# A two-pass causal attention layer: rows of maxima turned by VectorE in SBUF, whole value matmuls and filler matmuls in the diagonal steps

## The reference, cut to what matters

```python
x = x + attention(layernorm(x))
x = x + relu(layernorm(x) @ w1 + b1) @ w2 + b2

def attention(x):                      # 16 heads, d_k = 16
    Q, K, V = rope(x @ Wq.T), rope(x @ Wk.T), x @ Wv.T
    scores = Q @ K.T / 4               # causal: -inf above the diagonal
    return softmax(scores) @ V @ Wo.T
```

## Time and profile before

| | |
|---|---|
| Median of three runs | 2168.51 us |
| The profiled execution: its own time | 2172.91 us |
| Its span, first to last instruction | 2171.2 us |
| TensorE busy | 2008.1 us, 92% of the span |
| VectorE busy | 1902.2 us, 88% |
| ScalarE busy | 1457.4 us, 67% |
| GpSimd busy | 637.1 us, 29% |
| Mean granted TensorE clock | 0.967 of full speed |

### The profile page before, as it was taken

The page is one execution under the profiler, slowest core; times in us unless marked ns, Lnnn a source line. Parts: engine busy times, 40 slices in busy tenths (PEclk is TensorE's granted clock), DMA queues, the critical chain, the costliest instruction groups (busy, mean ns, idle before and its releaser), DMA issues. The chain is left out here.

```text
span 2171.2 us, 53576 instructions
## 1 busy us (share of the span) xinstructions
PE 2008.1 (92%) x19136; PEld 790.4 (36%) x19136; DVE 1902.2 (88%) x3974; ACT 1457.4 (67%) x3092; POOL 637.1 (29%) x1265
## 2 busy tenths in 40 slices
PE   5786599999999999999999999999999969999999
PEld 3444122222222222222222222222222237766776
DVE  8998899999999999999999999999999337777775
ACT  5664078888888788888888788888887742333222
POOL 7999421120221202221121211212212123332231
PEclk9999599999999999999999999999999889999999
DMA  5567331230313303033130322303120212222220
GB/s 193 203 220 209 122 70 37 51 65 17 72 27 64 61 22 66 21 76 50 33 66 17 76 35 52 66 17 74 27 52 13 69 39 78 82 94 84 87 78 29
DMA packets 126407, 152.64 MB, mean 70 GB/s; under 512 B 17248, under 2 KB 92512, under 8 KB 125920
## 3 DMA queue, kind: packets, MB, share of 16 engines
q1 hardware_dynamic: 126176, 149.67, 26.0%
HBM read 90.12 MB, written 59.24 MB: 69 GB/s over the span
## 5 line engine op out<-in xcount | busy, mean ns | idle before, releaser
L868 ACT ACTIVATE s_prob<-s_ps 128x512 f32<-128x512 f32 (+3 forms) x2560 | 1179.3, 540 | 276.5 <-PE s_ps L723 267.3
L797 DVE TENSOR_REDUCE s_part<-s_ps 128x2 f32<-128x1024 f32 x768 | 909.1, 1222 | 42.7 <-PE s_ps L706 25.1
L742 PE MATMUL s_ps<-s_prob,s_v 128*32 128x256 f32 (+3 forms) x10240 | 744.4, 363 | 8.4 <-POOL s_prob L898 0.9
L723 PE MATMUL s_ps<-aq,ak 64*128 64x512 f16 (+3 forms) x2560 | 674.5, 355 | 7.2 <-DVE s_part L804 1.2
L706 PE MATMUL s_ps<-mk,mq 64*128 64x512 f16 (+3 forms) x2560 | 590.7, 355 | 60.4 <-DVE s_part L797 28.1
L898 POOL TENSOR_SCALAR_AFFINE_SELECT s_prob<-s_prob 128x128 f32<-128x128 f32 x1024 | 286.7, 292 | 1170.7 <-ACT s_prob L868 1158.2
L804 DVE CUSTOM_DVE_ANT_0 s_ps<-s_ps,mask_sb 128x512 f32<-128x512 f32 (+3 forms) x1024 | 472.3, 520 | 25.9 <-PE s_ps L706 20.6
L723 PEld LDWEIGHTS s_ps<-aq,ak 64*128 64x128 f16 x2560 | 180.9, 93 | 524.0 <-ACT s_prob L868 439.9
L742 PEld LDWEIGHTS s_ps<-s_prob,s_v 128*32 128x32 f32 x10240 | 202.2, 108 | 464.4 <-issue 378.3
L706 PEld LDWEIGHTS s_ps<-mk,mq 64*128 64x128 f16 x2560 | 141.0, 95 | 105.4 <-DVE s_part L797 48.9
L1166 ACT ACTIVATE s_h_f<-s_ps,s_b_s 128x512 f32<-128x512 f32 x128 | 87.9, 687 | 105.9 <-PE s_ps L1031 85.0
(11 more groups left out here) (86 smaller groups left out, 1562.1 us busy)
## 6 DMA issues: line engine op xcount, KB each, us to landing
v_scratch<-s_vst SPq DMA_DIRECT2D x32, 512.0 KB, 3.9
s_v<-v_scratch SPq DMA_DIRECT2D x16, 1024.0 KB, 10.8
att_scratch<-s_o SPq DMA_DIRECT2D x64, 256.0 KB, 2.4
aq<-qk_scratch SPq DMA_DIRECT2D x96, 128.0 KB, 4.3
ak<-qk_scratch SPq DMA_DIRECT2D x96, 128.0 KB, 6.9
s_xin<-x SPq DMA_DIRECT2D x16, 512.0 KB, 4.4
qk_scratch<-s_r_lo SPq DMA_DIRECT2D x64, 128.0 KB, 2.2
qk_scratch<-s_r_hi SPq DMA_DIRECT2D x64, 128.0 KB, 2.4
```

The costliest lines, as they stand in the source:

```text
L723: nc.tensor.matmul(ps[:, s_bank(s, j), q0:CH], ak[rows, p, j // 2, kb * P:(kb + 1) * P], aq[rows, p, j // 2, c * CH + q0:(c + 1) * CH], st ...
L742: last = nc.tensor.matmul(ps[32 * j:32 * j + 32, O_BANK, cols], v[:, p, kb, j, :], prob[:, s % 2, j, cols], start=kb == 0 and part == 0, s ...
L797: nc.vector.tensor_reduce(part[:, qt // TPC, :, pair, qt % TPC, kc], ps[:, bank_of(use):bank_of(use) + 2, 0:w], AX.X, ALU.max).then_inc(m_ ...
L868: nc.scalar.activation(prob[:, s % 2, j, q0:CH], ps[:, s_bank(s, j), q0:CH], ACT.Exp, scale=1.0 / (SQK * DK ** 0.5)).then_inc(p_done, 1)
```

## The change

- `qmax` is reduced to a tile 32 columns wide, of which 16 are used, VectorE turns it in blocks of 32x32 in SBUF (`turn_chunk`) and scales it there (`rows_out`). TensorE's `max_rows` and its two uses of the ring are gone.
- The turned tile holds a chunk's rows in four pieces of 32 queries, so `rows` now issues eight DMAs of 64-byte pieces in place of four of 256-byte pieces. `aq` gets the layout `[NC, NP, CH]`, and its loads become twelve DMAs in place of six (18 in `load_a` in place of 12).
- In all diagonal steps the order on TensorE is: scores 0 and 1, first pair of maxima, score 2, second pair of maxima, score 3, and then the value matmuls whole, in place of two halves.
- In the diagonal steps of the tail, where there are no maxima, two pairs of 512-column matmuls that nobody reads are issued in their place (`filler_pair`).

```diff
-                dst = (ops.ak if qk else ops.aq)[rows, p]
-                sp.dma_start(dst, src[jj]).then_inc(ops.a_in[p], 16)
+                if qk:
+                    sp.dma_start(ops.ak[rows, p], src).then_inc(ops.a_in[p], 16)
+                    continue
+                for jp in range(NP):
+                    sp.dma_start(ops.aq[rows, p, :, jp], src[:, jp].rearrange("r (c t) -> r c t", c=NC)
+                                 ).then_inc(ops.a_in[p], 16)
...
-        self.aq = ctx.enter_context(nc.sbuf_tensor("aq", [P, 2, NP, S], F16))
+        self.aq = ctx.enter_context(nc.sbuf_tensor("aq", [P, 2, NC, NP, CH], F16))
...
-                sp.wait_ge(m_read, NM + rows_use(i, c) + ROWS_TILES)
-                for j in range(G):
-                    row = HROWS * (j % 2) + MAXROW
-                    k = TPC * (NP * (j % 2) + j // 2)
-                    sp.dma_start(aq[row:row + 1, i % 2, j // 2, c * CH:(c + 1) * CH], nrow[k:k + TPC, c, :]
-                                 ).then_inc(rows_in[c], 16)
+                sp.wait_ge(nrow_done, NC * i + RANK[c] + 1)
+                for jj in range(2):
+                    row = HROWS * jj + MAXROW
+                    dst = aq[row:row + 1, i % 2, c].rearrange("a n (q u x) -> a u (n q) x", u=P // TURN, x=TURN)
+                    for u in range(P // TURN):
+                        k = TURN * u + NP * TPC * jj
+                        sp.dma_start(dst[:, u], nrow[k:k + NP * TPC, c, :]).then_inc(rows_in[c], 16)
...
-            def max_rows(i, c):
-                use = rows_use(i, c)
-                pe.wait_ge(qmax_done, NC * i + RANK[c] + 1)
-                pe.wait_ge(m_read, use + ROWS_TILES)
-                nc.tensor.transpose(ps[0:G * TPC, bank_of(use), 0:P], qmax[:, c, :], ident[:]
-                                    ).then_inc(m_ready, ROWS_TILES)
+            def filler_pair(p, s, pair):
+                qt, kc = MAX_TILES[(s + LAG) % NS]
+                for jj in range(2):
+                    rows = slice(HROWS * jj, HROWS * (jj + 1))
+                    nc.tensor.matmul(ps[:, M_BANK + 2 * pair + jj], mq[rows, p, pair, qt * P:(qt + 1) * P],
+                                     mk[rows, p, pair, 0:CH], start=True, stop=True)
...
                     if t < STEPS_M:
                         max_pair(t, 0)
+                    elif is_diagonal(s):
+                        filler_pair(p, s, 0)
                     score_tile(i, p, s, 2)
-                    value_step(i, p, s, 0)
-                    score_tile(i, p, s, 3)
+                    if not is_diagonal(s):
+                        value_step(i, p, s, 0)
+                        score_tile(i, p, s, 3)
                     if t < STEPS_M:
                         max_pair(t, 1)
-                    value_step(i, p, s, 1)
-                    if t <= STEPS_M:
-                        for of, c in rows_after(t):
-                            max_rows(of, c)
+                    elif is_diagonal(s):
+                        filler_pair(p, s, 1)
+                    if is_diagonal(s):
+                        score_tile(i, p, s, 3)
+                        value_step(i, p, s, 0, 1)
+                    else:
+                        value_step(i, p, s, 1)
...
+            def turn_chunk(i, c):
+                dve.wait_ge(qmax_done, NC * i + RANK[c] + 1)
+                nc.vector.transpose(qmax_t[:, c, :], qmax[:, c, :]).then_inc(turned, 1)
+
             def rows_out(i, c):
-                use = rows_use(i, c)
-                dve.wait_ge(m_ready, use + ROWS_TILES)
+                dve.wait_ge(turned, NC * i + RANK[c] + 1)
                 dve.wait_ge(rows_in[c], 16 * ROWS_DMAS * i)
-                nc.vector.tensor_scalar(nrow[:, c, :], ps[0:G * TPC, bank_of(use), 0:P], -1.0 / SQK, None, ALU.mult
-                                        ).then_inc(m_read, ROWS_TILES)
+                nc.vector.tensor_scalar(nrow[:, c, :], qmax_t[:, c, :], -1.0 / SQK, None, ALU.mult).then_inc(nrow_done, 1)
```

More of the change, by code:

```diff
@@ L530, in sem @@
             return ctx.enter_context(nc.semaphore(name))
-        ident, mask = ops.ident, ops.mask
+        mask = ops.mask
+        TURN = 32
         mq, mk, aq, ak, m_in, a_in = ops.mq, ops.mk, ops.aq, ops.ak, ops.m_in, ops.a_in
@@ L535, in stage2 @@
         part = sb("s2_part", [P, NC, 2, NP, TPC, NC], F32)
-        qmax = sb("s2_qmax", [P, NC, G * TPC], F32)
-        nrow = sb("s2_nrow", [G * TPC, NC, P], F16)
+        qmax = sb("s2_qmax", [P, NC, TURN], F32)
+        qmax_t = sb("s2_qmax_t", [P, NC, TURN], F32)
+        nrow = sb("s2_nrow", [P, NC, TURN], F16)
         prob = sb("s2_prob", [P, 2, G, CH], F32)
@@ L566, in stage2, with ended @@
         STEPS_M = NIT * NS
[L568 to L575, removed]
+        RANK = [sum(e < MAX_END[c] for e in MAX_END) for c in range(NC)]
+        def ended(t):
+            return [(i, c) for i in (t // NS - 1, t // NS) for c in range(NC)
+                    if 0 <= i < NIT and t == NS * i + MAX_END[c]]
         def m_use(t, j):
[L579 to L584, removed]
+            return G * t + j
         def bank_of(use):
@@ L598, in read_before @@
             return ST * i + last_in_bank + 1
-        RANK = [sum(e < MAX_END[c] for e in MAX_END) for c in range(NC)]
         def crosses_diagonal(qt, kc):
@@ L723, in score_tile, with pv_step @@
                 nc.tensor.matmul(ps[:, s_bank(s, j), q0:CH], ak[rows, p, j // 2, kb * P:(kb + 1) * P],
-                                 aq[rows, p, j // 2, c * CH + q0:(c + 1) * CH], start=True, stop=True
+                                 aq[rows, p, c, j // 2, q0:CH], start=True, stop=True
                                  ).then_inc(s_ready, 1)
-            def pv_step(i, p, s, part):
+            def pv_step(i, p, s, part, parts=2):
                 c, kb = STEPS[s]
                 q0 = max(0, kb - TPC * c) * P
-                half = (CH - q0) // 2
+                size = (CH - q0) // parts
                 if part == 0:
@@ L738, in pv_step @@
                         pe.wait_ge(p_done, ST * i + G * s + G + G)
-                cols = slice(q0 + half * part, q0 + half * (part + 1))
+                cols = slice(q0 + size * part, q0 + size * (part + 1))
                 for j in range(G):
@@ L743, in pv_step, with value_step @@
                                             prob[:, s % 2, j, cols], start=kb == 0 and part == 0,
-                                            stop=kb == TPC * (c + 1) - 1 and part == 1)
-                if part == 1:
+                                            stop=kb == TPC * (c + 1) - 1 and part == parts - 1)
+                if part == parts - 1:
                     last.then_inc(pv_done, 1)
-            def value_step(i, p, s, part):
+            def value_step(i, p, s, part, parts=2):
                 if s > 0:
-                    pv_step(i, p, s - 1, part)
+                    pv_step(i, p, s - 1, part, parts)
                 elif i > 0:
-                    pv_step(i - 1, 1 - p, NS - 1, part)
+                    pv_step(i - 1, 1 - p, NS - 1, part, parts)
             def iteration(i, p, use):
@@ L760, in iteration @@
                     t = NS * i + s + LAG
+                    if t == STEPS_M:
+                        pe.wait_ge(m_read, NM + m_use(STEPS_M, 0))
                     if s in CHUNK_START:
@@ L832, in step @@
                     max_of_pair(t, 0)
-                if t <= STEPS_M:
-                    for of, c in rows_after(t):
-                        max_of_chunk(of, c)
+                for i, c in ended(t):
+                    max_of_chunk(i, c)
+                    turn_chunk(i, c)
+                    rows_out(i, c)
                 if t < STEPS_M:
                     max_of_pair(t, 1)
-                if t <= STEPS_M:
-                    for of, c in rows_after(t):
-                        rows_out(of, c)
             dve.sem_inc(m_read, NM)
             nc.vector.memset(part[:], -3e38).then_inc(part_preset, 1)
+            nc.vector.memset(qmax[:], 0.0).then_inc(qmax_preset, 1)
             dve.wait_ge(ops.const_in, 16)
             dve.wait_ge(part_preset, 1)
+            dve.wait_ge(qmax_preset, 1)
             for t in range(LAG):
```

20 lines of the change are left out of this document (8 added, 12 removed).

## The result

The kernel after takes 2283.2 us (median of 4 runs, 2277.79 to 2293.13), the kernel before 2167.88 in its four runs: ratio 1.0538, 95% interval 1.0499 to 1.0576. It is 115 us slower, where 2170 us and at most 2194 were forecast. The profiled execution took 2285.96 us.

The account below looks back on a forecast made before the run. TensorE was taken to bound ordinary steps, with VectorE equally tight in diagonal ones. Terms -20.8 + 14.9 + 8.7 + 6.0 - 6.7 - 0.6 = +1.5 us on 2168.5 gave 2170 us, range 2138 to 2194.

Parts of the forecast that it names:

- Part 1: Steps 5 and 25: without TensorE's turn of maxima they become ordinary steps, 0.67 us less, 31 times: -20.8 us.
- rival (c): Diagonal blocks: VectorE's own waits in chunk work cost 1.0 instead of 0.61 us, +12 us, 2182 us; chance 0.08.
- Part 2: Diagonal steps: new order costs +14.9 us in steps 8-11 and 36-39, +8.7 us in 0-3 and 20-23.
- Rival (a): Diagonal blocks: the new order costs nothing, they go at VectorE's pace, 2142 us; chance 0.36 with milder forms.
- Part 3: Start of step 4: rows by eight DMAs make it 0.4 us late, 15 times: +6.0 us, up to +21.
- rival (b): Chunks 1 and 2: rows land late or issues cost more, 15 x 1.4 us, 2191 us; chance 0.22.
- Hidden, with nothing to spare: Step 12: rows of chunk 2 land near 575.6, the step would start at 575.7; no wait charged.
- bytes ahead of it are unchanged: SyncE's queue, held first row issue of chunk 2: same bytes ahead; load_a starts 2.2 us later.
- A drop of the clock while the maxima run would be dearer; nothing speaks for it: Steps with maxima: a clock drop there was named as dearer than +6.7 us, without a size or chance.
- Part 4: Tail, behind step 23 of the last iteration: fillers hold the clock, -6.7 us if it works, 0 if not.
- Rival (d): Tail of the last iteration: the fillers don't hold the clock, +6.7 us, 2177 us; chance 0.10.

Follow-up runs that it names:

- the kernel whose rows are not awaited: Kernel after, with its row DMAs writing to a spare tile nobody reads and TensorE not waiting for them: 2174.27 us, ratio 1.0034.
- the loads behind the rows: Kernel after, with the next pair's loads issued behind the rows of chunk 2, all eight row DMAs kept: 2219.88 us, ratio 1.0238.
- the best version: Kernel after with four row DMAs, the old order of diagonal steps, and the next pair's loads behind the rows of chunk 2: 2133.22 us, ratio 0.9841.

## Why the prediction was wrong

**Part 1, the turn: right.** Steps 4 and 5 went from 87.9 to 76.5 us in the kernel whose rows are not awaited, 24 to 26 from 125.6 (with the tail at full clock) to 114.6: -22.4 us, forecast -20.8. Step 5 takes 2.37 us. VectorE's chunk work, which no row had shown:

```profile
572.05 0.21 DVE L813 TENSOR_REDUCE s_qmax<-s_part 128x16 f32<-128x64 f32 x1
572.30 0.21 DVE L818 STREAM_TRANSPOSE s_qmax_t<-s_qmax 128x32 f32<-128x32 f32 x1
572.55 0.18 DVE L823 TENSOR_SCALAR s_nrow<-s_qmax_t 128x32 f16<-128x32 f32 x1
572.71 0.70 DVE L805 CUSTOM_DVE_ANT_0 s_ps<-s_ps,mask_sb 128x512 f32<-128x512 f32 x1
```

From 572.05 to the next maximum it is 0.66 us, forecast 0.61 with bounds of 0.34 and 1.0; rival (c) is out. In the prediction the Trainium skill (VectorE: DVE Perf Modes, The three transpose paths) stood with 311 ns for a turn of 128x128 at 16 bits; the 128x32 one takes 0.21 us here, so its 3 us were not to be added.

**Part 2, the order: right.** Rows not awaited against before: 8.4 us in steps 8 to 11 and 6.6 in 36 to 39, together 15.0, forecast 14.9; 5.8 and 4.4 us in steps 0 to 3 and 20 to 23, 10.2 in place of 8.7. In the median these two blocks take 8.79 us for 8.51, +0.28 as forecast; the rest of the 10.2 is the clock, which fell in steps 1 to 4 of a few iterations of either kernel. The mechanism shows in the waits of the maxima for VectorE, after and before:

```profile
PE s_ps L702 <- DVE s_part L805: 35.4, 102, 0.7
```

```profile
PE s_ps L706 <- DVE s_part L804: 11.1, 37, 0.7
```

In steps 8 to 11 and 36 to 39 there is no such wait before that the profile counts, and after there are 4.4 us of it in each of the two, over all iterations. Rival (a) is out for the change as made.

**Part 3, rows by eight DMAs: this is the step that failed**, +6.0 us forecast, 116 measured (the 75.2 and 41.2 above). The rows came late, as rival (b) had it, but its 27 us in all were four times too small. Four terms were off.

- *The issues.* I took 0.617 us per row issue and 0.467 per load from the earlier trace rows. They take 5.39 / 8 = 0.67 and 7.67 / 12 = 0.64. That the loads change their shape with the layout, from six issues to twelve of another kind, I counted in number and not in price. The loads cost 7.67 - 2.77 = 4.9 us of queue, and only part of that came back in a shorter hold of the next issues.
- *The landing.* I took 1.4 us, the smaller of the earlier trace rows. Step 4's first score at 579.92 follows the last row issue (578.84 - 0.64 = 578.20) by 1.7 us. The Trainium skill (DMA: Bandwidth & Descriptors, Anatomy of one DMA) gives a DMA that GpSimd issues a fixed cost of about 2.0 us, of which most is the receipt of the write. These are issued by SyncE, and the trace lies midway between that and my 1.4. The 0.3 us were 4.5 us over 15 iterations, small beside the rest.
- *"Hidden, with nothing to spare".* For chunk 2 I forecast the last issue at 574.2, 25.0 us into the iteration. It comes at 598.3, 27.8 us into it: the held first issue is not let go 2.2 us later than before, as "bytes ahead of it are unchanged" had it, but about 4.5 (5.6 in the median of the iterations). Step 11 takes 4.67 us in the median for 1.51, and steps 8 to 11 together 41 us more over all iterations, the largest single item, priced at nothing. The earlier trace rows had the slack: step 12's first score came 5.6 us after the last row issue, and the landing needs 1.7. For chunk 3 I charged none of the four extra issues, about 2.7 us. Before, the first scores of steps 4 and 24 came 2.9 us after the last row issue, which leaves 1.2 beside a landing of 1.7; steps 20 to 23 cost 21 us.
- *What a wait does to the clock.* This was in no term. 41 us of the 116 are steps behind a wait, at granted clocks down to 0.50, while TensorE has work. The sentence "A drop of the clock while the maxima run would be dearer; nothing speaks for it" was wrong, and the trace of the kernel before speaks for it: in step 1 of iterations 5, 10 and 15 the clock is at 0.50 for 3.4 us, which costs 1.5 us each time. The earlier trace rows shows an iteration without one. Step 1 of iterations 4 and 5, before:

```profile
643.49:646.34 2.85, 2.53 (x27) 0.81 (x27) 2.60 (x10) 1.85 (x6) 1.17 (x4) 1.00 0.27 98
735.29:739.45 4.16, 3.85 (x27) 0.98 (x27) 2.92 (x11) 1.85 (x5) 1.17 (x4) 0.61 0.18 66
```

The change put three idle stretches of about 1 to 3 us into each iteration, and the clock fell behind 22 of these 45. The Trainium skill (TensorE: Matmul & The Clock Gate, HAM oscillation) describes a loop of this kind, in which the wait for each tile's data throttles the next one, with waits of 3 to 5 us. The trace agrees in that the clock falls behind waits, with 7.11 us for steps 12 and 13 in place of 4.76, but here most waits are shorter and only half of them are followed by a fall.

**Part 4, the tail: wrong in size and in kind.** The profiled execution of before has a slow tail (7.7 us in the table, against the others), but most runs seem not to. The mean granted clock of the profiled one was 0.967, and of the 15 runs of before that stand beside the fillers' 14 lie at 0.969 to 0.973 with 2165 to 2171 us and one at 0.967 with 2174. The 4.4 us by which the profiled one lay above the median were the sign. A loss that the runs don't have can't be won back in them; fillers alone gave 1.0006, and two of their eleven runs stand at 0.967 and 0.968 with 2175 and 2176 us. The prediction found the trace in line with activity that releases the clock; but in the same window the clock stood at 0.51 with TensorE busy for 18.96 of 19.00 us, and filled steps 20 to 23 were followed by 1.00 in one kernel and by 0.66 in another. The slow tail also makes up 7.7 of the 12 us between the table, where the kernel with rows not awaited is 4.0 us shorter than before, and the runs, where it is 8 us longer. The other 4 are that kernel's own profiled execution, 4.0 us below its median. Rival (d) named the case, at 6.7 us.

Together: the profiled execution was forecast at 2174.4 and took 2285.96, 111.6 us more; 110.4 of them are part 3 (116.4 - 6.0). In this pair of profiled executions the -6.7 of part 4 look right, as the tail gained 7.7, but that is luck: kernels with and without fillers have it either way.

## What to carry to other kernels

Count the issues of a DMA queue with their shapes, as for an engine: for each transfer that somebody waits for, write down how long before its reader it is issued, and take what is added ahead of it off that slack, chunk by chunk. "Nothing to spare" is a forecast of a wait and needs a price. An idle stretch of TensorE of a microsecond or more costs its own length and can cost slow steps behind it: on average half as much again in the kernel after (41.2 us for 75.2), a third with the loads behind the rows (11.3 for 34.5), and 0.7 of it with eight row DMAs in the kernel before (23.9 for 33.3). And when a sum holds one loser, keep the winner: merged DMAs kept the turn's gain without the wait.

## What the runs showed that I had not expected

- The issue cost on SyncE depends on the shape: four partitions in the row DMA of before 0.617 us, two partitions in its halves 0.60, eight partitions in pieces of 64 bytes 0.67, sixteen partitions in the best version 0.54 (1.61 us from the first to the fourth of chunk 2), the six loads 2.77 / 6 = 0.46, the twelve with an extra dimension 0.64, though each of these moves half the bytes. The landing of the twelve is shorter than that of the six of before, 2.6 us against 4.3. The keys' loads, which did not change, also land sooner, in 4.4 us where they took 6.9. First before, then after:

```profile
aq<-qk_scratch SPq DMA_DIRECT2D x96, 128.0 KB, 4.3
ak<-qk_scratch SPq DMA_DIRECT2D x96, 128.0 KB, 6.9
```

```profile
aq<-qk_scratch SPq DMA_DIRECT2D x192, 64.0 KB, 2.6
ak<-qk_scratch SPq DMA_DIRECT2D x96, 128.0 KB, 4.4
```

- Two kernels whose steps 20 to 23 are alike to 0.01 us go on at a granted clock of 0.61 and of 1.00. A single execution can't price such a tail.
- Two delays in one queue that cost 9 and 65 us alone go with 109 us in the kernel after, and hid a gain: the same turn by VectorE is part of the version at 0.9841.
